# Forward chunks around masks of 128 columns in group 3, and GpSimd's first sum ahead of eight blocks

## What is computed

```
h  = relu(layernorm(x))
s  = (h @ W) @ a[:64];  t = (V @ W) @ a[64:]
e  = leaky_relu(s[i] + t[j], 0.2), and -9e15 where adj[i, j] == 0
x1 = x + elu(softmax(e, axis=1) @ V + h)
h2 = relu(layernorm(x1))
out = x1 + relu((adj^T @ h2) @ U^T / deg),   deg = adj.sum(axis=0)
```

## Time and profile before

| what | us |
|---|---|
| median of three runs | 369.61 |
| the profiled execution | 369.23 |
| its span, first to last instruction | 367.4 |
| TensorE matmul busy | 305.9 (83%) |
| VectorE busy | 299.6 (82%) |
| ScalarE busy | 267.0 (73%) |
| GpSimd busy | 124.1 (34%) |

### The profile page before, as it was taken

How to read it: one execution, slowest core, us unless ns; L and a number is a source line. 1 busy time by engine, 2 the same in 40 slices (tenths; PEclk the granted TensorE clock), 3 DMA queues, 4 the chain that set the end, 5 groups by cost and what they waited for, 6 DMA issues and landing times.

```text
span 367.4 us, 15473 instructions
## 1 busy us (share of the span) xinstructions
PE 305.9 (83%) x7140; PEld 276.1 (75%) x7140; DVE 299.6 (82%) x403; ACT 267.0 (73%) x392; POOL 124.1 (34%) x120
## 2 busy tenths in 40 slices
PE   1816766677889878989899999997989999999995
PEld 1712555466668667878779998886989998999995
DVE  7889999896999779999978589999989786403964
ACT  2377999799998899999989899995787785101000
POOL 8857898487141582120115130004102010301000
PEclk9956899999989999999999999999999999999999
DMA  8999999999999999999401021000111103510211
GB/s 162 140 111 108 109 108 110 136 108 109 108 110 141 103 108 105 103 103 105 87 6 33 26 72 41 26 17 26 38 27 34 40 25 70 118 30 9 51 34 30
DMA packets 28766, 27.82 MB, mean 76 GB/s; under 512 B 22209, under 2 KB 24065, under 8 KB 28702
## 3 DMA queue, kind: packets, MB, share of 16 engines
q0 software_dynamic: 4752, 16.90, 44.2%
q1 hardware_dynamic: 21790, 9.39, 10.5%
q10 hardware_dynamic: 2160, 0.56, 0.9%
HBM read 74.08 MB, written 3.43 MB: 211 GB/s over the span
## 4 chain that ended last, share of the span: by engine, by line
PE 34%; DVE 29%; POOL 15%; issue 11%; ACT 8%; DMA 4%; POOLq 0%; DVEq 0%
DVE scratch L947 19%; PE w L1323 11%; PE q L1410 9%; PE q L1295 6%; DVE arena L1009 5%; POOL adj_sb L486 5%; PE w L1410 5%; DMA adj_sb<-in_adj_dram 4%; ACT q L792 3%; ACT arena L778 3%; POOL buf_b L546 2%; POOL adj_sb L490 2%; POOL stat_c L589 2%; ACT arena L774 2%; POOL g_all L563 2%
## 5 line engine op out<-in xcount | busy, mean ns | idle before, releaser
L1323 PE MATMUL w<-v_sb,arena 128*61 128x65 f32 (+1 forms) x4224 | 156.4, 224 | 1.8 <-ACT arena L778 1.7
L947 DVE CUSTOM_DVE_ANT_0 scratch<-adj_sb,t_row 125x2048 uint8<-125x2048 uint8 x66 | 153.4, 2324 | 3.1 <-DMA adj_sb<-in_adj_dram 1.7
L1323 PEld LDWEIGHTS w<-v_sb,arena 128*64 128x64 f32 (+1 forms) x4224 | 138.6, 137 | 9.8 <-ACT arena L778 2.9
L1295 PE MATMUL q<-bi,adj_sb 128*64 128x125 bf16 (+1 forms) x1664 | 91.5, 222 | 32.5 <-ACT q L792 30.4
L1295 PEld LDWEIGHTS q<-bi,adj_sb 128*64 128x64 fp8e4 (+1 forms) x1664 | 66.8, 108 | 47.3 <-ACT q L792 38.4
L774 ACT ACTIVATE arena<-q,t_col 128x1000 f32<-128x1000 f32 (+2 forms) x101 | 87.4, 871 | 0.1
L778 ACT ACTIVATE arena<-arena,t 128x1000 f32<-128x1000 f32 (+2 forms) x59 | 64.2, 1088 | 21.6 <-DVE arena L1009 21.0
L1009 DVE SCALAR_TENSOR_TENSOR arena<-arena,b_col,q 128x1000 f32<-128x1000 f32 (+1 forms) x44 | 52.9, 1210 | 11.0 <-PE q L1295 7.5
L792 ACT ACTIVATE q<-second_row,minus_b 128x750 f32<-128x750 f32 (+1 forms) x49 | 47.8, 976 | 1.1
L792 ACT ACTIVATE q<-arena,minus_b 128x375 f32<-128x375 f32 (+1 forms) x52 | 41.8, 804 | 1.3
L598 POOL TENSOR_TENSOR g_all<-buf_a,g_all 125x512 f16<-125x512 f32 (+2 forms) x5 | 7.9, 1581 | 80.1 <-ACT buf_a L756 80.1
(11 more groups left out here) (150 smaller groups left out, 255.4 us busy)
## 6 DMA issues: line engine op xcount, KB each, us to landing
adj_sb<-in_adj_dram POOLq DMA_DIRECT2D x33, 500.0 KB, 41.4
saved_dram<-x_sb SPq DMA_DIRECT2D x6, 193.5 KB, 2.5
t_row<-saved_dram SPq DMA_DIRECT2D x6, 193.5 KB, 2.4
arena<-s_dram SPq DMA_DIRECT2D x2, 500.0 KB, 7.4
out_dram<-v_sb SPq DMA_DIRECT2D x10, 96.0 KB, 1.8
x_sb<-in_x_dram SPq DMA_DIRECT2D x1, 928.0 KB
v_sb<-x_dram SPq DMA_DIRECT2D x1, 768.0 KB, 5.5
v_sb<-n_L_gnn_entity_embs_dram ACTq DMA_DIRECT2D x2, 256.0 KB, 5.7
```

Of the source, the lines that this page charges most:

```text
L947: nc.vector.tensor_tensor_reduce(out=junk[0:R, :], in0=adj_bytes[0:R, b, half], in1=t_row[0:R, half], scale=1.0 / ONE, scalar=0.0, op0=ALU ...
L1295: last = nc.tensor.matmul(q[n % Q_SLOTS][e:e + width, bank, start:start + R], weights, bi[:, i % BI_SLOTS, k, :], start=not ON_ACT[n] and ...
L1323: last = nc.tensor.matmul(att(i)[e0:e1, bank, place_in, :], e[:, k * R + e0:k * R + e1], v_sb[:, c, :], start=(c == 0 and place_in == 0), ...
```

## The change

The masks of a tile of group 3 with chunks are one of 128 columns per block instead of two of 64. Half of the tile's chunks (one of two, none of one) go ahead of the mask, the rest between mask and attend. The 20 chunks stand in 13 tiles, two in seven of them and one in six; before they stood in 16 tiles. GpSimd's sum of group 0 goes ahead of blocks 21 to 28, the other three closing steps stay behind them. Some shares and places of steps differ too.

```diff
-    DVE_TILES = [(28, 30, 31),
-                 (25, 27, 29, 31),
-                 (1, 7, 9, 12, 18, 23, 27, 29, 30, 31),
+    DVE_TILES = [(29, 30, 31),
+                 (0, 25, 28, 30),
+                 (1, 7, 9, 12, 18, 23, 27, 29, 31),
...
-    GUARD_TILES = [(4, 8, 9, 11, 11, 14, 14, 17, 19, 20, 20, 24),
-                   (1, 1, 3, 4, 4, 6, 6, 7, 9, 10, 12, 14, 19, 20, 21, 21),
-                   (2, 4, 6, 9, 10, 14, 14, 16, 17, 21, 21, 21, 22, 23, 24, 26),
-                   (4, 11, 13, 14, 14, 15, 16, 17, 17, 17, 20, 21, 21, 22, 23, 24)]
+    GUARD_TILES = [(4, 8, 11, 11, 11, 14, 14, 17, 19, 20, 21, 24),
+                   (1, 1, 3, 4, 4, 4, 6, 7, 9, 10, 13, 15, 19, 20, 21, 21),
+                   (3, 3, 6, 9, 10, 14, 14, 16, 17, 21, 21, 21, 22, 23, 24, 26),
+                   (4, 11, 13, 14, 14, 15, 16, 17, 17, 19, 20, 21, 22, 22, 23, 24)]
...
-        'elu': (None, 4, 7, 3, 8),
+        'elu': (None, 4, 7, 3, 9),
-        'spread': (None, 12, 12, 12, 13),
+        'spread': (None, 10, 12, 12, 13),
-        'copy_h2': (None, 20, 17, 19, 18),
+        'copy_h2': (None, 20, 17, 19, 17),
-        'turn_r': (27, 27, 29, 28, None),
-        'copy_r': (29, 28, 29, 27, None),
+        'turn_r': (27, 27, 29, 29, None),
+        'copy_r': (28, 28, 29, 29, None),
-        'variance_0': (10, None, None, None, None),
+        'variance_0': (8, None, None, None, None),
-        'turn_s': (13, 11, 9, 12, None),
+        'turn_s': (13, 10, 9, 12, None),
...
-    AHEAD_TILES = (3, 4, 4, 7, 8, 10, 12, 13, 13, 15, 17, 17, 18, 20, 21, 22, 23, 25, 28, 28)
-    AHEAD_COPIES = (5, 11, 13, 17, 21, 26, 31)
+    AHEAD_TILES = (3, 3, 5, 7, 7, 9, 11, 11, 13, 15, 15, 17, 18, 18, 20, 22, 22, 24, 26, 26)
+    AHEAD_COPIES = (6, 10, 14, 17, 21, 25, 28)
...
-                elif b in (13, 21):
-                    pool.wait_ge(h1_weighted, {13: 2, 21: 3}[b])
+                elif b == 13:
+                    pool.wait_ge(h1_weighted, 2)
+                elif b == 21:
+                    pool.wait_ge(hpg_done, 1)
...
                 pool.wait_ge(g_done, min(i + 2, NI))
+                if i == 0:
+                    pool.wait_ge(h1_weighted, 3)
...
             weigh_h(2)
+            close_sum(0)
             for b in range(21, 29):
                 set_ones(b)
                 load(b)
-            close(0)
+            close_centre(0)
+            close_power(0)
+            close_low(0)
...
-                width = MASK_COLUMNS[i]
+                width = P if i == AHEAD_IN and c in AHEAD_TILES else MASK_COLUMNS[i]
...
             for n, (i, c) in enumerate(TILES):
+                ahead = [chunk for tile, chunk in zip(AHEAD_TILES, chunks_ahead) if tile == c and i == AHEAD_IN]
+                for chunk in ahead[:len(ahead) // 2]:
+                    sum_ahead(*chunk)
                 mask(n, i, c)
+                for chunk in ahead[len(ahead) // 2:]:
+                    sum_ahead(*chunk)
                 if n >= 2:
                     attend(n - 2, *TILES[n - 2])
-                if i == AHEAD_IN:
-                    for tile, chunk in zip(AHEAD_TILES, chunks_ahead):
-                        if tile == c:
-                            sum_ahead(*chunk)
```

## The result

Four runs of the changed kernel took 372.98, 373.0, 374.19 and 374.47 us, median 373.6; the kernel before took 369.09 beside them (368.4 to 369.84). The medians are 4.5 us apart; the recorded ratio, which is not the quotient of these two medians, is 1.0107 (1.0071 to 1.0143): slower. The forecast was 373.2. The profiled execution took 374.47 us, its span 372.6 (before: 367.4). Single executions of the kernel before, of c and of d further down took 431 to 464 us at a granted clock of 0.59 to 0.66 and are left out of the ratios.

The account below looks back on a forecast made before the run. No engine alone bound groups 1 to 3; in group 3 TensorE set the pace to tile 12, then VectorE. Terms -2.9 + 4.8 + 1.9 = +3.8 us on 369.23, adjusted to 373.2 us; range 371.5 to 375.

Parts of the forecast that it names:

- The start of group 3: Groups 0 to 2: mainly removed waits bring group 3's first mask earlier, -2.9 us (bounds -4.5 and -0.5).
- -0.6 for the tiles of group 0: Group 0: tile 28 goes to ScalarE, so its wait for VectorE's scores shrinks, -0.6 us.
- the loss in group 2: Group 2: tile 30 goes from VectorE to ScalarE, whose extra relu costs +0.45 us at the hand-over.
- The sentences on the skill: Group 1: port shared with busy VectorE stretches the moved sum to 2.5 us; ScalarE waits some 0.4 us again.
- Group 3 up to scores 12: Group 3: chunks wait for ScalarE's bank copies ahead of masks 7 and 11, mask 12 +4.8 us later.
- +0.75: Group 3 ahead of mask 12: eight chunks instead of six in five tiles cost TensorE +0.75 us, within the +4.8.
- 1.4 us of TensorE saved, hidden: Group 3: fewer chunk tiles and wide masks save TensorE 1.4 us, hidden in the half where VectorE sets the pace.
- The halves: End of group 3: later copy of the halves delays group 4's first mask, +1.9 us (bounds +0.3 and +2.2).
- (a): Rival: group 3's waits for copies do not bite, only gains stay, 367.5 to 369.4 us; chance 0.20.
- (b): Rival: full VectorE gain of 4.5 us, no waits, TensorE's 1.4 us kept, 363.7 us; chance 0.07.
- (c): Rival: group 2, with three full engines, swallows group 1's gain, 375.8 us; chance 0.16 together with (d).
- (d): Rival: the sum is on time but later loads starve, at most +4.9 us; chance 0.16 together with (c).

Follow-up runs that it names:

- c: Changed kernel with ScalarE's bank copies one tile earlier and the halves' transpose and copy back at tiles 28 and 27; median 370.39 us, ratio 1.0018.
- d: Changed kernel with group 3's old chunk places, bank copies, 64-column masks and hand-over; only edits of groups 0 to 2 stay; median 368.05 us, ratio 0.9961.
- e: Kernel before with only GpSimd's sum of group 0 moved ahead of blocks 21 to 28; median 367.85 us, ratio 0.995.
- i: d with the scaling in group 3 at tile 14 instead of 13; median 366.1 us, ratio 0.9906.
- j: i with ScalarE's copies of h2 @ U in group 3 at tile 26 instead of 27; median 365.58 us, ratio 0.9896.
- k: e with group 3's scaling at tile 14, times_u at 24 instead of 25 and high at 25 instead of 27; median 364.92 us, ratio 0.987.
- b: Changed kernel with the transpose and copy of the halves for group 4 back at tiles 28 and 27; median 372.3 us, ratio 1.0059.
- a: Changed kernel with ScalarE's bank copies in group 3 one tile earlier; median 370.86 us, ratio 1.0041.
- m: k with GpSimd's 125x512 closing step of group 3 made to wait until VectorE's row shifts are done; median 364.46 us, ratio 0.9857.
- h: c with all masks of group 3 in halves of 64 columns; median 370.14 us, ratio 1.0031.
- l: c with five chunks instead of eight ahead of mask 12 in group 3; median 368.08 us, ratio 0.9965.

## Why the prediction was right

**The start of group 3: -2.9, measured -1.96, of which 1.35 are the change's (2.40 for the sum alone).** The steps at GpSimd and VectorE came out: sum at 80.18, 0.55 us, the 3.25 us gone, group 1 shorter by 2.5. Late loads cost nothing. By the start of group 2 the sum had brought 2.67 us (e). Wrong were two terms beside it. The -0.6 for the tiles of group 0 is not there at the start of group 2 (82.55 us from the guard with these edits, 82.50 without). And the loss in group 2, put at +0.4, was 1.27 (64.15 for 62.88 us, first mask to first mask), of which the sum alone has 0.27; the likely place of the other 1.0 is VectorE's step that centres x (L872), 1.63 us for 0.69. The text also holds a slip: it takes the tiles of group 1 at 0 and still writes -0.5 into the sum. All of the gain is the sum's (e); the edits around it took 1.03 us of it back (d).

**Port.** The sentences on the skill let the moved sum take 2.5 us beside a busy VectorE. It took 0.55: it started beside a reduction (79.92), and the guard that began while it ran (80.51) took 2.35 us for 2.29. So here the sum was not held. The centring behind it took 2.45 us beside a guard, as before. The Trainium skill, "SBUF — State Buffer", Terms, says of the shared port pair that the engine that loses it is blocked for the whole of the other's instruction. The row shifts agree: those that begin while GpSimd's step runs end with it (0.17 us alone, 0.96 to 0.99 in the kernel before, i and j), and in k a guard took 0.79 us more.

**Group 3 up to scores 12: +4.8, measured +6.48, of which 1.54 is a slow clock.** The chain exp, copy, chunk, mask was stepped through rightly (+1.89 and +2.36 for +2.1 and +2.4; +4.96 at mask 12 for +4.8), and b, with the same waits and the clock at full speed, has +4.94 at s12. The +0.75 in it for two more chunks was mis-sized: with the waits nearly gone (a) the stretch is 1.93 us longer than before. 0.80 of that are the two waits that a still has (0.30 and 0.50), and 1.1 the two chunks and the passages (by the costs per tile it would be 3 x 1.36 + 2 x 0.80 - 1.29 - 4 x 0.79 = 1.2). The error was to credit the wide masks with savings per tile. Old tiles cost 0.79 and 1.29 over a plain one, new ones 0.80 and 1.36.

**"1.4 us of TensorE saved, hidden".** It is hidden, but it isn't there. Seven tiles of two chunks and six of one cost 7 x 1.36 + 6 x 0.80 = 14.3 us over plain ones; the old list, four of two and twelve of one, 4 x 1.29 + 12 x 0.79 = 14.6. The saving is 0.3 us.

**Scores 12 to 28: 0, measured -0.79.** The mechanism, VectorE alone, is right (i). Not seen was that GpSimd's closing step falls on a row shift in the kernel before (the 0.96 stood in its timeline) and beside scores in the changed one.

**The halves: +1.9, measured +1.73.** Copy at 261.19, mask 2.51 us behind its end, 1.51 of them waited for the DMA. b gives 1.7 us back.

**The rivals.** (a), the waits don't bite: with the waits nearly gone and the halves as before (c) the median is 370.39 and the lowest time 369.1, where the rival had 367.5 at that end; its -2.15 had the same -2.9 and +0.75 in it, both too good (-1.35 and about +1.2). (b) needed the point at which VectorE no longer sets the end of group 3; that came only in m, after 2.4 us had been taken from VectorE. (c), group 2 swallows the gain, was partly so: 1.27 us of it, and for the most part through the other edits. (d) is out: loads that left 4.3 us later landed as before (42.1 us from issue, 41.4 before), and no engine waited for them.

With the slow clock and the late start of the kernel before taken out, the stretches are -1.35, +4.94, -0.79, +1.73 and -0.26, together +4.3 for a forecast of +3.8. The errors by stretch are +1.5, +0.1, -0.8, -0.2 and -0.3. The direction and the two large terms of group 3 were foreseen; that the sum came out within 0.5 us is partly luck, since a gain at the start that was put twice too high was made up for by a collision in the kernel before that nobody had counted.

## What to carry to other kernels

Ask which engine sets the end of each stretch, and put extra work for another engine in the stretch where it doesn't: three chunks moved behind tile 12 cost nothing, two moved ahead of it cost 1.1 to 1.2 us. Steps moved along with the one that matters are not free: here they took back 1.0 of its 2.4 us. A buffer's copy that stands one tile ahead of its next use becomes a wait on a chain of mask, scores, exp and copy, however idle the copying engine is. A row of 0.96 us where its like take 0.17 is worth a look at the other engine's row at that moment, and the cure may be to put the other's step later, beside work that it doesn't hold.

## What the runs showed of the hardware

- **The clock after a stand-still.** In the changed kernel TensorE stood still for 1.97 us before chunk 11; the clock granted in the next stretches was 0.73 and then 0.50 of full speed, that is 1.2 GHz, until 218.3 us, where it returned to 0.92 and more. In b the same stand-still of 1.96 us was followed by full speed, in c one of 2.10 us by 0.54 to 0.56 for 3.8 us. Such a stretch cost 1.5 us up to s12, where TensorE sets the pace (28.60 for 27.06 in b, 25.56 in c for 24.05 in a).
- **The spread of one kernel's times.** The changed kernel took 373.0 twice, and 374.2 and 374.5; the kernel before 368.4 and 368.6, and 369.6 and 369.8. The slow clock can be the reason in the changed kernel: its two faster executions had a mean clock of 0.981, the profiled one 0.972. It is not the only one. The profiled execution of b is one of the slower (372.3, the lowest 371.3) with full speed behind the stand-still, and it was 1.03 us behind before group 0 began, 0.9 of it by a wait for a block. In c executions of 370.4 us had a higher mean clock (0.981) than the one of 369.1 (0.971). What each run lost is not shown; only profiled executions tell.
- **Plain and custom steps of VectorE beside GpSimd.** Plain steps of 125x8 that begin while GpSimd's 125x512 step runs end with it (in the profiles of before, a, c, d, e, h, i and j: 0.96 to 1.04 us for 0.17 to 0.23). The guard, a custom step that takes 2.29, took 3.08 us where GpSimd's step ran for the first 0.94 us of it, and 2.35 where the moved sum ran for its first 0.22. The scores, which read PSUM, were not held where they were seen beside it: in m 1.25 us beside 1.12 us of GpSimd's, and none longer than usual in the changed kernel and in l.
- **A small DMA inside the core** (the halves, 16x125 bf16) took 2.65 us at the start of group 3 in before, after and e, and 2.51 at the start of group 4 in the changed kernel, from the end of the copy that feeds it to the matmul that needs it; in c's profiled execution it was 4.15.
